# Two transformer blocks on one core: POOL's square roots moved ahead of its weight work, one operation of the rotation moved to ScalarE, the mean correction moved to VectorE, and multiplications of zeros before the first FFN

## The chip, the cores and the metric

One core of one Trainium2 chip. The metric is device time in microseconds (us); lower is better. Engines: PE is TensorE, with PEld for its weight loads, DVE is VectorE, ACT is ScalarE, POOL is GpSimd, SP is SyncE (here it issues DMAs). Each has its own instruction stream, runs it in order, and waits for the others through semaphores.

## The reference

Four sequences of 256 tokens of width 256, float32, through two blocks:

```python
xn = layernorm(x)
x = x + attn0(xn, w_norm, w_qkv, w_out, pm) + ffn0(xn, weight, bias, gamma, beta)
xn = layernorm(x)
x = x + attn1(xn, w_qkv, w_o) + ffn1(xn, w_fc, w_proj)
```

`attn0` has windows of two tokens with 16 learned keys. `ffn0` is one ternary matrix. `attn1` has 32 query heads and 4 key/value heads of 64, with rotary positions, causal:

```python
def _rope(x, pos):
    x1, x2 = jnp.split(x, 2, axis=-1)
    return jnp.concatenate([x1 * cos - x2 * sin, x2 * cos + x1 * sin], axis=-1)
```

`ffn1` is layer norm, quantized input, ternary 256 x 1024, exact GELU, layer norm again, ternary 1024 x 256.

## The kernel before

The order of every engine is written out by hand, with semaphores between the engines. To keep float32 accuracy with the fast matmul format, operands are split: ACT writes a rounded half (`hi`), and another engine subtracts it from the full value (`lo`).

**Front.** PE makes the products of block 0's attention and ffn (`g_products`, `m_products`, `ffn_0(b)`, `attention_0(b)`); DVE adds each batch to x (`add0(b)`) and takes its layer statistics (`stats1(b)`); POOL raises the variance to -1/2 (`batch_root(b)`, through `root`, L593); ACT normalises (`normal1(b)`, L473); PE transposes (`turn_tokens(b)`); ACT and DVE split the result (`tokens_hi`, `tokens_lo`). Beside this ACT turns weights ternary (`sign`, L407), sums |w_proj| (L452) and rounds the attention weights in 18 parts (`weights_hi`, L463), from which POOL makes `lo` parts (`weights_lo`, L607), in the same order.

**FFN of block 1.** Ten steps, a tile of 128 tokens in each. PE: `hidden_T(t)`, `fc(step)` (L1114), `proj(t-1)` (L1138) and a projection for the attention (`fill`, L1179). ACT: `hidden_hi`, `gelu`. DVE: `hidden_stats(t)`, `hidden_lo(t)`, `hidden_factors(t)` (L877, needs POOL's `tile_root(t)`), `ffn_add(t-1)` (L888). PE's `proj(t)` waits for `ffn_add(t-1)`.

**Attention of block 1.** 16 iterations (batch, key head) of 6 slots; 96 slots in all. In slot n PE makes scores of unit n (L1229), transposes the probabilities of unit n-2 (L992), multiplies a group of units by the values (L1266), and at some slots projects the outputs (L1286) or fills bank 6 with a new projection. ACT's slot: `probs_T(n-2)` (L528), exponents `probs(n)` (L519), group copy, `raw` copy of the fill (L494). DVE's slot: `maxima(n)` (L910), `normalise(n-1)` (L926), `probs_lo(n-2)` (L932), group `lo`.

**Rotation.** The fills are 36 blocks of queries or keys, 32 of them from slots: a q block at slots 6it and 6it+3, a k block at slots 10, 34 and 58. For block n: `raw` copy on ACT, SP moves the half heads (`turned`, four DMAs), POOL multiplies twice (`rope_products`, L648 and L650), then in `rope_sums` writes the sum rounded (`split_hi`, L658), the sum full (L659), and the difference (`split_lo`, L660); SP places both (`place_heads`, four DMAs for q, eight for k). Buffers are double: the `raw` copy of block n waits for the products of block n-2. A q block is used 9 slots after its fill. In its loop POOL takes after each of blocks 4 to 11 up to two weight parts and one `mean_part` (L671 and L674: x += wcol * factor, for the mean that the second layer norm subtracts).

Of the kernel before, what the change touches and what calls it, by code (L numbers as in the profile page):

```python
# [9 lines left out]
BF16 = mybir.dt.bfloat16  # L10
# [4 lines left out]
P = 128  # L15
# [15 lines left out]
UNITS = 6  # L31
# [34 lines left out]
def build(nc, seq, w_qkv0, w_out0, pm, w_ffn0, bias0, w_qkv1, w_o1, w_fc, w_proj, vec, const, out):  # L66
    with ExitStack() as ctx:
# [36 lines left out]
        def at(name, offset, shape, dt=F32):  # L104
# [58 lines left out]
        mcol = at("mcol", 187 * K, [P, DIM])  # L163
# [16 lines left out]
        lo0_done = sem("lo0_done")  # L180
        tern_in, nb_done, ones_done, wcol_full, wcol_done, f_mean, mean_made = (
            sem(n) for n in ("tern_in", "nb_done", "ones_done", "wcol_full", "wcol_done", "f_mean", "mean_made"))
# [12 lines left out]
        raw_done, rope_done, split_done = sem("raw_done"), sem("rope_done"), sem("split_done")  # L195
# [15 lines left out]


# [4 lines left out]
        def fills_at(it, u):  # L217
# [8 lines left out]
            if u == 4 and g == 2 and b + 1 < B:  # L226
# [4 lines left out]
        HI_IN = {0: 4, 1: 5, 2: 6, 3: 7, 4: 8, 5: 9, 6: 10, 7: 12}  # L231
# [4 lines left out]
                + [f for it in range(ITS) for u in range(UNITS) for f in fills_at(it, u)])  # L236
        PREPARED = sum(map(len, FILLS_IN.values()))
# [160 lines left out]
        def _(act):  # L398
# [25 lines left out]
            def whole_x(b):  # L424

                for k in range(KC):
# [18 lines left out]
            nc.scalar.activation(ones_r[:, :], cst[:, C_ONE:C_ONE + P], ACT.Copy).then_inc(ones_done, 1)  # L445
            act.wait_ge(p0_T, 1)
# [3 lines left out]
            sign(1, nat_fc[:, :, :], fcT[:, :, :], tern_fc)  # L450
            act.wait_ge(ld["proj"], 16)
            nc.scalar.activation(abs_out[:, :], nat_proj[:, :, :].rearrange("p c n -> p (c n)"), ACT.Abs,  # L452
                                 accum_out=wsum[:, 2:3]).then_inc(proj_sum, 1)

# [91 lines left out]
            weights_hi(0, 3)  # L546
# [32 lines left out]
        def _(pool):  # L579
# [49 lines left out]
            weights_lo(0, 2)  # L629
            batch_root(0)  # L630
            weights_lo(2, 3)
# [20 lines left out]
            def rope_sums(n):  # L652
# [13 lines left out]
            def mean_part(t):  # L666

                if t == 0:
                    pool.wait_ge(wcol_done, 1)
                pool.wait_ge(f_add, t + 1)  # L670
                pool.tensor_tensor(mcol[:, :], wcol[:, :], ffac[:, t, 4:5].to_broadcast([P, DIM]), ALU.mult).then_inc(mean_made, 1)  # L671
                pool.wait_ge(mean_made, t + 1)
                part = x[:, t // 2, t % 2, :]
                pool.tensor_tensor(part, part, mcol[:, :], ALU.add).then_inc(f_mean, 1)  # L674
                pool.wait_ge(f_mean, t + 1)

            batch_root(3)
            weights_lo(3, 4)
            tile_root(0)
            weights_lo(4, 5)  # L680
            pool.wait_ge(ld["rope"], 16)
            rope_products(0)
            tile_root(1)
            rope_sums(0)
            tile_root(2)
            rope_products(1)
            tile_root(3)
            rope_sums(1)
            tile_root(4)
            rope_products(2)  # L690
            tile_root(5)
            rope_sums(2)
            weights_lo(5, 6)
# [4 lines left out]
            weights_lo(6, 9)  # L698
# [9 lines left out]
        def _(dve):  # L708
# [27 lines left out]

            dve.memset(blk_k[:, :], 0.0).then_inc(blk_zero, 1)
# [627 lines left out]
```

## Time and profile before

| | us |
|---|---|
| median of 3 runs | 406.86 (406.72 to 406.94) |
| the profiled execution | 406.81 |
| its span | 405.0 |
| PE busy | 369.5 (91%) |
| DVE busy | 303.5 (75%) |
| POOL busy | 285.9 (71%) |
| ACT busy | 251.1 (62%) |

The chain that ended last is PE for 66% of the span, POOL for 18%, DVE for 6%. Times in rows are from the start of the span. "Idle before" and the name behind the arrow tell how long an engine waited and what ended the wait. Matmuls are pipelined, so successive starts, not the lengths of single ones, give their pace. The granted clock is a share of 2.4 GHz: 1.00 is 2.4 and 0.50 is 1.2 GHz.

### The profile page before, as it was taken

Reading aid. Unit: us, or ns where it says so; the run is one execution under the profiler, and the core shown is the slowest. Engines: PE = TensorE matmul, PEld = TensorE weight load, DVE = VectorE, ACT = ScalarE, POOL = GpSimd, SP = SyncE. Lnnn points to the kernel's source line nnn. Section 1 sums busy time; section 2 is a strip of 40 time slices with the busy share of each in tenths; the row PEclk is TensorE's granted clock in tenths of the full one; section 3 lists DMA queues with packets and bytes.
Section 4 is the critical chain, followed back from the end, with each engine's and each line's share of the span. In section 5 each row is a group of like instructions: output and inputs, shape, how many; then the busy total and the mean of one; then the engine's idle time right before and its main releaser. Section 6 shows DMA issues by size and latency. Waiting matters only on the chain.

```text
span 405.0 us, 8415 instructions
## 1 busy us (share of the span) xinstructions
PE 369.5 (91%) x2852; PEld 347.6 (86%) x2868; DVE 303.5 (75%) x675; ACT 251.1 (62%) x808; POOL 285.9 (71%) x250
## 2 busy tenths in 40 slices
PE   3994686999999979699999999999999999999995
PEld 1664574999889979699999999999999999998985
DVE  4876596786787658467977887787778778787883
ACT  1346466347598465466776757677775758677671
POOL 3445337647999999999877987677798867777000
PEclk9998699899999989879999999999999999999999
DMA  8995010522333333534434563443447344433200
GB/s 262 413 408 217 1 32 21 130 55 68 79 89 94 81 77 81 135 84 95 116 79 104 137 161 91 100 104 91 100 113 180 88 98 95 110 85 78 79 2 26
DMA packets 34219, 45.15 MB, mean 111 GB/s; under 512 B 5505, under 2 KB 25986, under 8 KB 33794
## 3 DMA queue, kind: packets, MB, share of 16 engines
q1 hardware_dynamic: 34032, 44.62, 41.2%
q8 instruction: 23, 0.38, 0.4%
q14 instruction: 18, 0.15, 0.1%
q10 hardware_dynamic: 146, 0.00, 0.0%
HBM read 13.14 MB, written 1.05 MB: 35 GB/s over the span
## 4 chain that ended last, share of the span: by engine, by line
PE 66%; POOL 18%; DVE 6%; ACT 3%; issue 3%; DMA 3%; SPq 1%; POOLq 0%
PE bank L1266 14%; PE bank L1229 11%; PE bank L992 10%; PE bank L1286 10%; PE bank L1179 9%; PE bank L1138 3%; POOL woT_lo L607 2%; PE bank L1114 2%; POOL split_lo L660 2%; POOL split_hi L658 2%; POOL rope_b L650 2%; POOL rope_a L659 2%; POOL qkvT_lo L607 2%; PE bank L1232 2%; POOL rope_a L648 2%
## 5 line engine op out<-in xcount | busy, mean ns | idle before, releaser
L519 ACT ACTIVATE bank<-bank,neg_max 128x256 f32<-128x256 f32 (+1 forms) x256 | 101.3, 397 | 6.0 <-DVE neg_max L910 5.8
L528 ACT ACTIVATE probT_hi<-bank 128x512 fp32r<-128x512 f32 x96 | 57.6, 600 | 74.2 <-PE bank L992 74.1
L910 DVE TENSOR_REDUCE neg_max<-bank 128x2 f32<-128x512 f32 (+1 forms) x96 | 66.0, 688 | 38.2 <-PE bank L1232 26.7
L1266 PE MATMUL bank<-probT_hi,v 128*128 128x256 f32 x384 | 76.7, 296 | 3.1 <-DVE probT_lo L932 2.4
L1229 PE MATMUL bank<-kT,qT 128*128 128x256 f32 (+1 forms) x512 | 75.1, 280 | 3.2 <-DMA qT<-split_lo 3.2
L650 POOL TENSOR_TENSOR rope_b<-turned,cst 128x512 f32<-128x512 f32 x36 | 46.4, 1290 | 36.2 <-DMA turned<-raw 36.1
L1229 PEld LDWEIGHTS bank<-kT,qT 128*128 128x128 f32 x512 | 68.3, 196 | 3.4 <-DMA qT<-split_lo 3.4
L932 DVE TENSOR_TENSOR probT_lo<-bank,probT_hi 128x512 fp32r<-128x512 f32 x96 | 65.4, 681 | 5.3 <-ACT probT_hi L528 5.2
L926 DVE TENSOR_TENSOR prob<-bank,rsum 128x512 f32<-128x512 f32 x96 | 66.4, 691 | 3.3
L1266 PEld LDWEIGHTS bank<-probT_hi,v 128*128 128x128 f32 x384 | 58.8, 190 | 6.2 <-DVE probT_lo L932 3.8
L992 PE MATMUL bank<-cst,prob 128*128 128x128 f32 x384 | 58.6, 276 | 3.1 <-DVE prob L926 2.1
L1266 PE MATMUL bank<-probT_lo,v 128*128 128x256 f32 x192 | 54.2, 283 | 0.0
L519 ACT ACTIVATION_READ_ACCUMULATOR bank<-bank,neg_max 128x1 f32 x256 | 53.8, 210 | 0.0
L992 PEld LDWEIGHTS bank<-cst,prob 128*128 128x128 f32 x384 | 46.6, 143 | 5.1 <-DVE prob L926 2.6
L660 POOL TENSOR_TENSOR split_lo<-rope_a,split_hi 128x512 fp32r<-128x512 f32 x36 | 46.2, 1283 | 2.8
L658 POOL TENSOR_TENSOR split_hi<-rope_a,rope_b 128x512 fp32r<-128x512 f32 x36 | 46.2, 1284 | 2.5
L648 POOL TENSOR_TENSOR rope_a<-raw,cst 128x512 f32<-128x512 f32 x36 | 46.4, 1289 | 0.6
L659 POOL TENSOR_TENSOR rope_a<-rope_a,rope_b 128x512 f32<-128x512 f32 x36 | 46.4, 1289 | 0.0
L938 DVE TENSOR_TENSOR oT_lo<-bank,oT_hi 128x256 fp32r<-128x256 f32 x64 | 27.2, 425 | 18.4 <-ACT oT_hi L533 18.3
L494 ACT ACTIVATE raw<-bank 128x512 f32<-128x512 f32 x36 | 21.8, 606 | 28.5 <-PE bank L1179 20.0
L1266 PEld LDWEIGHTS bank<-probT_lo,v 128*128 128x128 f32 x192 | 36.4, 190 | 0.0
L1179 PE MATMUL bank<-xT_hi,qkvT_hi 128*128 128x256 f32 x144 | 30.7, 295 | 2.9 <-DVE x L822 2.9
(155 smaller groups left out, 746.5 us busy)
## 6 DMA issues: line engine op xcount, KB each, us to landing
turned<-raw SPq DMA_DIRECT2D x144, 64.0 KB, 2.0
qT<-split_hi SPq DMA_DIRECT2D x64, 128.0 KB, 2.4
qT<-split_lo SPq DMA_DIRECT2D x64, 128.0 KB, 2.4
wq0T<-in_L_attn_w_qkv_dram SPq DMA_DIRECT2D x4, 512.0 KB, 8.2
wout<-in_L_attn_w_out_dram SPq DMA_DIRECT2D x4, 512.0 KB, 12.7
nat_qkv<-in_L_attn_w_qkv_dram SPq DMA_DIRECT2D x2, 1024.0 KB, 20.9
nat_o<-in_L_attn_w_o_dram SPq DMA_DIRECT2D x1, 2048.0 KB, 21.6
kT<-split_hi SPq DMA_DIRECT2D x16, 128.0 KB, 2.4
```

The lines of the kernel that those rows point to most:

```text
L519: ins = nc.scalar.activation(own, own, ACT.Exp, bias=neg_max[it % 2][:, first + j:first + j + 1], accum_out=sums[it % 2][:, first + j:firs ...
L528: nc.scalar.activation(probT[0][:, n % 4, :], bank[2 + n % 2][:, :], ACT.Copy).then_inc(t_hi, 1)
L648: pool.tensor_tensor(a, whole, cos, ALU.mult)
L650: own_done(pool.tensor_tensor(z, half, sin, ALU.mult))
L659: own_done(pool.tensor_tensor(a, a, z, ALU.add))
L910: dve.tensor_reduce(neg_max[n // UNITS % 2][:, unit_columns(n % UNITS)], score_bank(n)[:, :].rearrange("p (h k) -> p h k", h=heads), AX.X, ...
L926: dve.tensor_tensor(a, e, share, ALU.mult).then_inc(s_norm, 1)
L932: dve.tensor_tensor(lo, bank[2 + n % 2][:, :], hi.bitcast(F32), ALU.subtract).then_inc(t_lo, 1)
L992: ins = pe.transpose(ps[:, P * j:P * j + P], a, ident)
L1179: ins = pe.matmul(bank[place][:, SEQ * j:SEQ * j + SEQ], qkvT[w][:, k, at:at + P], xT[s][:, k, SEQ * b:SEQ * b + SEQ], start=i == 0, stop= ...
L1229: pe.matmul(ps[:, keys * j:keys * j + keys], qT[it % 2][:, h + j, P * c:P * c + P], kT[b % 2][:, g, s, 0:keys], start=j == 0 and s == 0, s ...
L1266: ins = pe.matmul(group_bank(), v[b % 2][:, DH * z:DH * z + P], p, start=m == 0, stop=m == last)
```

## The change

1. POOL takes `weights_lo` in other portions: one part before the root of batch 0, two before that of batch 1, and later parts between roots. The root of batch 3 comes behind parts 3 and 4.
2. ACT takes one weight part before `sign(1)` and the absolute sum, two after; the load of the GELU table comes before `probT0`.
3. DVE adds batches 2 and 3 to x before `hidden_scale(0)` and `tokens_lo(0)`. `hidden_factors` stands one step later, right before `ffn_add`.
4. From block 4 on ACT, not POOL, writes `split_hi`, as a copy of POOL's full sum, in the slot four after the block's fill, between `probs_T` and `probs`. POOL waits for it before `split_lo`. Blocks 0 to 3 stay as they were.
5. `mean_part` becomes one DVE operation at the head of slots 6 to 13.
6. PE multiplies a zeroed tile of 512 columns (bfloat16) into unused banks: 14 times at the start, 6 times before and 5 times after the transposes of batch 0, which now stand behind `ffn_0(3)` and `attention_0(3)`.

```diff
@@ ScalarE
+            nc.scalar.activation(table_use[:, 0:1], table_use[:, 1:2], ACT.Gelu)
             act.wait_ge(p0_T, 1)
...
+            def high_rotated(n):
+                act.wait_ge(rope_done, summed(n))
+                if n >= 2:
+                    has_landed(act, n - 2)
+                nc.scalar.activation(split[0][:, n % 2, :, :], rope_a[:, n % 2, :].rearrange("p (j t) -> p j t", j=2),
+                                     ACT.Copy).then_inc(split_hi, 1)
             def slot(n):
                 if 2 <= n < N_UNITS + 2:
                     probs_T(n - 2)
+                for f in BLOCKS[OWN_HIGH:]:
+                    if FILL_SLOT[f] + 4 == n:
+                        high_rotated(BLOCK[f])
...
-            nc.scalar.activation(table_use[:, 0:1], table_use[:, 1:2], ACT.Gelu)
-            weights_hi(0, 3)
+            weights_hi(0, 1)
+            sign(1, nat_fc[:, :, :], fcT[:, :, :], tern_fc)
+            act.wait_ge(ld["proj"], 16)
+            nc.scalar.activation(abs_out[:, :], nat_proj[:, :, :].rearrange("p c n -> p (c n)"), ACT.Abs,
+                                 accum_out=wsum[:, 2:3]).then_inc(proj_sum, 1)
+            weights_hi(1, 3)
@@ GpSimd
-            weights_lo(0, 2)
+            weights_lo(0, 1)
             batch_root(0)
-            weights_lo(2, 3)
+            weights_lo(1, 3)
...
-                pool.tensor_tensor(hi, a, z, ALU.add)
+                if n < OWN_HIGH:
+                    pool.tensor_tensor(hi, a, z, ALU.add)
                 own_done(pool.tensor_tensor(a, a, z, ALU.add))
+                if n >= OWN_HIGH:
+                    pool.wait_ge(split_hi, n - OWN_HIGH + 1)
                 pool.tensor_tensor(lo, a, hi.bitcast(F32), ALU.subtract).then_inc(split_done, 1)
...
-                weights_lo(2 * n + 1, min(2 * n + 3, len(W_UNITS)))
-                if n - 4 < TILES:
-                    mean_part(n - 4)
+                weights_lo(2 * n + 2, min(2 * n + 4, len(W_UNITS)))
@@ VectorE
+            dve.memset(idle_in[:, :], 0.0).then_inc(idle_ready, 1)
...
             stats1(1)
+            add0(2)
+            add0(3)
             hidden_scale(0)
...
+                dve.scalar_tensor_tensor(part, wcol[:, :], ffac[:, t, 4:5], part, ALU.mult, ALU.add).then_inc(f_mean, 1)
             def slot(n):
+                if 6 <= n < 6 + TILES:
+                    mean_part(n - 6)
...
-                    hidden_factors(t)
+                if t >= 1:
+                    hidden_factors(t - 1)
+                    ffn_add(t - 1)
@@ TensorE
+            def keep_busy(b, count):
+                for _ in range(count):
+                    pe.matmul(bank[b][:, :], idle_in[:, 0:P], idle_in[:, :], start=True, stop=True)
+            pe.wait_ge(idle_ready, 1)
+            keep_busy(5, 14)
...
-            turn_tokens(0)
             ffn_0(3)
             attention_0(3)
+            keep_busy(4, 6)
+            turn_tokens(0)
+            keep_busy(2, 5)
```

## Rows read from the trace of the kernel before

**Rows 1.** Stages: stretch, length, busy us (instructions) of PE, PEld, DVE, ACT, POOL; clock; DMA

```profile
34.00:42.00 8.00, 1.36 (x7) 0.82 (x6) 5.50 (x19) 5.13 (x9) 4.81 (x5) 0.67 0.17 72
...
52.00:67.50 15.50, 14.89 (x96) 12.75 (x96) 11.55 (x39) 12.81 (x24) 8.92 (x9) 1.00 0.14 35
67.50:71.20 3.70, 0.01 (x1) 0.05 (x1) 3.63 (x7) 1.26 (x2) 3.05 (x3) 0.95 0.00 0
...
76.10:106.00 29.90, 29.90 (x225) 28.42 (x222) 21.59 (x58) 17.74 (x34) 21.21 (x20) 1.00 0.27 62
...
176.50:405.00 228.50, 222.21 (x1852) 215.98 (x1862) 178.99 (x360) 152.75 (x544) 159.34 (x127) 1.00 0.41 97
```

**Rows 2.** The chain that ended last, front: start us, length us, engine, tile, line

```profile
39.59 0.98 POOL tok L593
...
46.54 2.10 PE bank L1114 x8
...
71.19 3.49 PE bank L1138 x16
...
76.12 0.87 PE bank L992 x8
...
78.85 1.90 PE bank L1138 x16
```

**Rows 3.** Timeline, 25 to 40 us: start us, length us, engine, line, operation

```profile
27.49 0.59 ACT L447 ACTIVATE probT<-bank 64x512 f32<-64x512 f32 x1 [1.39 <-PE bank L1082]
...
31.10 2.00 ACT L407 ACTIVATE fcT<-nat_fc,neg_magic 128x2048 fp32r<-128x2048 f32 x1 [1.36 <-DVE nat_fc L773]
...
34.80 0.16 DVE L719 TENSOR_SCALAR tok<-tok 128x2 f32<-128x2 f32 x1
...
35.02 1.28 ACT L545 ACT_TABLE_LOAD   x1
...
36.42 1.65 ACT L463 ACTIVATE qkvT_hi<-nat_qkv 128x512 fp32r<-128x512 f32 x3
```

**Rows 4.** Timeline of POOL and of DVE, the same moment

```profile
40.79 1.26 POOL L607 TENSOR_TENSOR qkvT_lo<-nat_qkv,qkvT_hi 128x512 fp32r<-128x512 f32 x1
...
40.79 1.28 DVE L841 TENSOR_TENSOR tok<-tok 128x2 f32<-128x2 f32 x1
```

**Rows 5.** Groups by line: busy us, mean ns of one, idle before and its releaser

```profile
L650 POOL TENSOR_TENSOR rope_b<-turned,cst 128x512 f32<-128x512 f32 x36 | 46.4, 1290 | 36.2 <-DMA turned<-raw 36.1
...
L494 ACT ACTIVATE raw<-bank 128x512 f32<-128x512 f32 x36 | 21.8, 606 | 28.5 <-PE bank L1179 20.0 <-POOL rope_b L650 8.5
...
L607 POOL TENSOR_TENSOR woT_lo<-nat_o,woT_hi 128x512 fp32r<-128x512 f32 x8 | 10.2, 1283 | 0.0
...
L674 POOL TENSOR_TENSOR x<-x,mcol 128x256 f32<-128x256 f32 x8 | 5.9, 735 | 0.6
...
L671 POOL TENSOR_TENSOR mcol<-wcol,ffac 128x256 f32<-128x256 f32 x8 | 4.9, 613 | 0.0
...
L888 DVE SCALAR_TENSOR_TENSOR x<-bank,ffac,x 128x256 f32<-128x256 f32 x8 | 3.8, 481 | 5.2 <-PE bank L1138 5.2
```

**Rows 6.** Timeline of PE in the attention: slots 13, 14, a wait, slot 15, slot 21

```profile
138.23 0.64 PE L1229 MATMUL bank<-kT,qT 128*128 128x256 f32 x4
...
140.71 1.01 PE L1229 MATMUL bank<-kT,qT 128*128 128x128 f32 x8
...
144.80 0.50 PE L1266 MATMUL bank<-probT_hi,v 128*128 128x256 f32 x2 [2.41 <-DVE probT_lo L932]
...
146.65 1.80 PE L1229 MATMUL bank<-kT,qT 128*128 128x128 f32 x8
...
170.93 1.97 PE L1229 MATMUL bank<-kT,qT 128*128 128x128 f32 x8 [3.21 <-DMA qT<-split_lo]
```

**Rows 7.** Timeline of ACT, a `raw` copy in the attention

```profile
142.94 0.60 ACT L494 ACTIVATE raw<-bank 128x512 f32<-128x512 f32 x1 [4.87 <-POOL rope_b L650]
```

**Rows 8.** Timeline of POOL, before its loop over the later blocks

```profile
105.21 2.51 POOL L607 TENSOR_TENSOR qkvT_lo<-nat_qkv,qkvT_hi 128x512 fp32r<-128x512 f32 x2
```

More of the change, by code:

```diff
@@ L162, in build @@
         wcol = at("wcol", 186 * K, [P, DIM])
-        mcol = at("mcol", 187 * K, [P, DIM])
+        idle_in = at("idle_in", 187 * K, [P, 512], BF16)
         abs_out = at("abs_out", 164 * K, [P, FF // P * DIM])
@@ L194, in build @@
         v_zero = sem("v_zero")
-        raw_done, rope_done, split_done = sem("raw_done"), sem("rope_done"), sem("split_done")
+        raw_done, rope_done, split_done, split_hi = sem("raw_done"), sem("rope_done"), sem("split_done"), sem("split_hi")
         turn_landed = [sem(f"turn_landed{i}") for i in range(2)]
@@ L209, in build, with summed @@
         STEPS = TILES + 2
+        def summed(n):
+            return 2 * n + 2
         def of_batch(it):
@@ L236, in build @@
                 + [f for it in range(ITS) for u in range(UNITS) for f in fills_at(it, u)])
+        OWN_HIGH = sum(f[0] != "v" for fs in FILLS_IN.values() for f in fs)
+        FILL_SLOT = {f: UNITS * it + u for it in range(ITS) for u in range(UNITS) for f in fills_at(it, u)}
         PREPARED = sum(map(len, FILLS_IN.values()))
@@ L664, in tile_root @@
                 root(ffac[:, t:t + 1, 1:2], t + B + 3)
[L666 to L675, printed above, removed]
+            weights_lo(3, 5)
             batch_root(3)
-            weights_lo(3, 4)
-            tile_root(0)
-            weights_lo(4, 5)
             pool.wait_ge(ld["rope"], 16)
             rope_products(0)
+            tile_root(0)
+            rope_sums(0)
             tile_root(1)
-            rope_sums(0)
+            weights_lo(5, 6)
+            rope_products(1)
             tile_root(2)
-            rope_products(1)
+            rope_sums(1)
             tile_root(3)
-            rope_sums(1)
+            weights_lo(6, 7)
+            rope_products(2)
             tile_root(4)
-            rope_products(2)
+            rope_sums(2)
             tile_root(5)
-            rope_sums(2)
-            weights_lo(5, 6)
+            weights_lo(7, 9)
             tile_root(6)
@@ L697, in _ @@
             rope_sums(3)
-            weights_lo(6, 9)
+            weights_lo(9, 10)
             for n in range(4, len(BLOCKS)):
@@ L945, in add_out, with mean_part @@
                 dve.tensor_tensor(dst, dst, bank[BANK_OUT][:, :].rearrange("p (e n) -> p e n", e=2), ALU.add).then_inc(out_added, 1)
+            def mean_part(t):
+                if t == 0:
+                    dve.wait_ge(wcol_done, 1)
+                dve.wait_ge(f_add, t + 1)
+                part = x[:, t // 2, t % 2, :]
+                dve.scalar_tensor_tensor(part, wcol[:, :], ffac[:, t, 4:5], part, ALU.mult, ALU.add).then_inc(f_mean, 1)
             def slot(n):
+                if 6 <= n < 6 + TILES:
+                    mean_part(n - 6)
                 if n % (HKV * UNITS) == UNITS and n > HKV * UNITS:
@@ L959, in slot @@
                     empty(fills_at(n // UNITS, n % UNITS))
-            add0(2)
             stats1(2)
             tokens_lo(1)
-            add0(3)
             stats1(3)
@@ L977, in _ @@
                     hidden_scale(step + 1)
-                if t >= 1:
-                    ffn_add(t - 1)
                 empty(FILLS_IN.get(step, ()))
```

12 lines of the change are left out of this document (4 added, 8 removed).

## The prediction

> **What bounds the kernel now.** I read the stages first, then the chain, then the single waits. The stage table [rows 1] shows a kernel that TensorE (PE) bounds in two long stretches, 76.1 to 106 us (busy 29.90 of 29.90) and 176.5 to the end (222.21 of 228.50, the rest mostly at its tail). Only what stands before 76.1 us and between 138 and 176 us can be shortened by reordering.
>
> In front, PE is busy 1.36 us of 34 to 42 and 0.01 us of 67.5 to 71.2 [rows 1]. The chain [rows 2] says why. The root of batch 0 starts at 39.59, while VectorE (DVE) had its argument at 34.80 + 0.16 = 34.96 [rows 3]: GpSimd (POOL) takes `weights_lo(0, 2)` first, and these wait for ScalarE (ACT), which is behind `sign(1)`, the absolute sum and a table load of 1.28 us. The first `fc` then starts at 46.54. The second hole is circular: DVE stands at `hidden_factors(1)` until POOL has taken `tile_root(1)`, which is queued behind weights and rotation; PE waits for the `ffn_add` behind it. The projection that follows takes 3.49 us for 16 matmuls where a later one takes 1.90 [rows 2]: its clock fell to 1.2 GHz after the hole.
>
> In the attention POOL is the late one. A block with two weight parts and a mean part costs it 5 x 1.29 + 2 x 1.28 + 0.61 + 0.74 = 10.4 us [rows 5], while PE asks for one about each 8.7 us (two per iteration; an iteration is 17.4 us when nothing waits). PE meets that as 2.41 us at 144.80 and 3.21 us at 170.93 [rows 6], the first through ACT, whose `raw` copy waited 4.87 us for a rotation [rows 7].
>
> **Roots first and the heating matmuls: -10.4 us.** Three steps.
>
> (a) ACT keeps only one weight copy ahead of `sign(1)`. It falls into the 1.36 us that ACT waits there anyway [rows 3]; the table load goes into the 1.39 us before `probT0` and overshoots by about 0.1, which nobody waits for. Both are costed at nothing; without their covers they would be 0.5 and 1.3 us. ACT then ends sum and two copies at 36.1. POOL has no weights pending, roots at 35.0, and `normal1(0)` starts at 36.3 (before: 39.59 + 1.3). That is 4.5 us.
>
> (b) `y1` is written at 37.4. PE is then in `ffn_0(3)`, `attention_0(3)` and `keep_busy(4, 6)`. A 512-column matmul is 2.10/8 = 0.26 us [rows 2], so six are up to 1.6 and end near 38.5; the transposes wait about a microsecond for them. That is what the heating costs, and it brings a warm clock: the eight products of `ffn_0(3)` and the four transposes ran cold before. ACT copies, and DVE reaches `tokens_lo(0)` at 41.0, because `add0(2)`, `add0(3)` and `hidden_scale(0)` are now queued ahead of it. First `fc` at 41.7: 4.8 us earlier.
>
> (c) Up to the transposes of tile 3 (76.12 before [rows 2]) PE and POOL no longer hold anybody: the roots have a whole step, as `hidden_factors` stands one step later, and `ffn_add(0)` needs no late root. What is late next is DVE. From 52 to 67.5 it is busy 11.55 of 15.5 us [rows 1], and from `tokens_lo(0)` to `hidden_lo(2)` it has about 20 us of work, 1 us of waiting for others, and some three port waits of about 1 us. So 41.7 + 24 = 65.7, and 76.1 - 65.7 = 10.4 us. Bounds: 12 with no port wait, 8.5 with five.
>
> DVE and POOL hinder one another: a two-column product took 1.28 us while POOL ran a subtraction of 1.26 us from the same instant [rows 4].
>
> The 14 matmuls at the start cost nothing on the path: 14 x 0.26 x 2 = 7.3 us at the lower clock at most, and the first `g_products`, 3.6 us even then, end before or at 10.7 us or so, when the next weights have landed; bound 0 to 1. The zeroing of `idle_in` runs in DVE's wait for `pm`. From 76.1 to 106 PE is the bound in both kernels: no change.
>
> **The attention: -4.1 us, then +2.6.** POOL loses the sum it wrote as `split_hi` (1.29) and the mean parts (0.61 + 0.74), and starts the loop with one weight part where three stood (-2.5 us of the three that run from 105.21 on [rows 8]; the other two are taken earlier, in POOL's waits). A block costs it 4 x 1.29 + 2 x 1.28 = 7.7 us, later 5.2, below PE's 8.7.
>
> But the copy now sits in ACT's queue at the slot four after the fill, between `probs_T` and `probs`. It waits for POOL's sum, and everything ACT does waits with it; in turn POOL's `split_lo` waits for ACT's slot. Fills come three slots apart except the k blocks, which come one slot after a q block. Slot 13 to 14 is 140.71 - 138.23 = 2.48 us [rows 6]. Between the two copies POOL must do `split_lo`, two weights, two products and a sum: 1.28 + 2.56 + 2.58 + 1.29 + about 0.3 = 8.0 us. On the clock of the kernel before: copy of block 7 at 139.9, sum of block 8 at 148.0, ACT at that copy from 142.9, so it stands 5.2 us. PE needs the result two slots on, at 140.71 + 2 x 2.95 + 0.6 = 147.2; it gets it after the copy (0.5), four exponents (1.4) and DVE's reciprocal and product (0.95), at 150.9: idle 3.75 us, and a cold stretch behind it. After 2.41 us of idling eight score matmuls took 1.80 us for 1.01 [rows 6]; after the two longer waits the loss was 1.6 (3.49 - 1.90) to 2.7 us. I take 2. The first k block costs 5.8 us.
>
> The mean parts add 8 x 0.48 us to DVE in slots 6 to 13 (by the `ffn_add` form [rows 5]), and both its inputs lie in SBUF, so each can wait for POOL as in [rows 4]: 0 to 1.28 us. With half of that, 8 x 1.1 = 9 us goes into some 5 us of idle time and 2 us of pipeline; I add 1.2 us (0 to 4). The SBUF — State Buffer page of the Trainium skill (Who interferes with whom) says the second of two such operations blocks fully until the first ends; the rows agree, and with every mean part meeting a whole POOL operation its rule would put the DVE term near 4 us, 2.8 above mine.
>
> In the kernel before, slots 14 to 20 would last 21.8 us at the lengths that the same slots have one iteration later, so slot 21 would start at 162.5 and not at 170.93 [rows 6], and it took 2.7 us longer than 2.95 itself: 11.1 us lost. 11.1 - 7.0 = 4.1 us are won.
>
> The later k blocks (slots 34 and 58) have no weights between: 5.4 us of POOL work from one copy to the next sum, against 2.5 us plus ACT's place in its slot. ACT stands 2.7 us, of which some 1.4 is slack: 1.3 us of PE each, 2.6 in all, where the kernel before had none. Bounds: 0, and 4 each if the clock falls too. The 32 copies themselves (0.6 us as the `raw` copy [rows 5], 0.5 in spacing) lie in ACT's waits for PE: at nothing; on the path they would be 16 us.
>
> **Sum.** Profiled execution 406.81 (span 405.0 and 1.8 around it; the median, 406.86, is the same): 406.8 - 10.4 - 4.1 + 2.6 = 394.9. The k blocks' DMAs (eight in SP's queue, ahead of the next `turned`) can hold the next block by about 1 us more; I say 395.5.
>
> **Rivals.**
> *A, POOL and ACT never hold PE.* The copies find their sums ready, k blocks included: 406.8 - 10.4 - 11.1 = 385.3, to 389 with small waits. For it: POOL's load falls below PE's pace. Against: the 8.0 us in a 2.5 us gap. 14%.
> *B, the new wait is a second POOL bound.* Each k block cools PE and delays the next two blocks through SP: 8, 4 and 4 us, front gain at 8.5: 406.8 - 8.5 - 3.1 + 8 = 403.2. For it: the 3.2 us wait was enough for the lower clock. Against: later k blocks carry no weights. 18%.
> *C, slower: the copy lands on the path in every block.* ACT does the copy between two steps of the loop scores, exponent, share, transposes; if the loop has less than 0.5 us slack, 28 to 32 copies cost 14 to 16 us: 395.5 + 14 = 409.5. It decides at about 0.4 us per copy. Against: PE is nearly gapless from 176.5 on [rows 1] with ACT busy 152.75 of 228.5. 5%.
> *D, the front wins nothing net:* the roots come early but the clock stays low and DVE stays the bound: 406.8 - 3 - 4.1 + 2.6 = 402 to 406.5. 4%.
>
> **How the numbers follow.** The forecast (389 to 401) has 59%. The range to hold 8 in 10 reaches into A and B: 388.5 to 401.5. The measurement can tell about 0.2% (0.8 us) from no change. Faster by more: 0.92; within: 0.02; slower: 0.06.
>
> **What would show it.** The root of batch 0 at 35 us and `normal1(0)` near 36.3; the first `fc` near 41.7; no PE wait over 2 us from 42 to 66, and the 16 projections of tile 1 at 1.9 us; the transposes of tile 3 near 65.7. In the attention `raw` waits for no rotation; instead ACT's copy into `split_hi` waits for POOL's sum, longest (about 5 us) at the first k block, near 132 us on the new clock, and 2 to 3 us at the two others. Wrong would be: PE holes spread over all blocks (C), or none (A).

## The result, and the profile after

The change made the kernel slightly slower, by 0.6%: 409.6 us median (408.28 to 411.75) against 407.02 (406.34 to 409.5) for the kernel before beside it, a ratio of 1.0056, 95% interval [1.0032, 1.008]. The forecast was 395.5 with a range of 388.5 to 401.5. The profiled execution took 410.91 us, its span is 409.1 (before: 406.81 and 405.0), so it lies 1.3 us above its median, and the one before 0.2 below.

The first and the last scores of the attention split the span into three parts. From the timeline of PE, the kernel before and then the kernel after (start us, length us, engine, line, operation; slots 0 and 95):

```profile
101.18 0.52 PE L1229 MATMUL bank<-kT,qT 128*128 128x256 f32 x3
...
390.92 0.64 PE L1229 MATMUL bank<-kT,qT 128*128 128x256 f32 x4
```

```profile
94.20 0.52 PE L1256 MATMUL bank<-kT,qT 128*128 128x256 f32 x3
...
395.05 0.52 PE L1256 MATMUL bank<-kT,qT 128*128 128x256 f32 x3
```

The attention begins 7.0 us earlier and takes 300.85 us instead of 289.74, 11.1 more; 11.1 - 7.0 = 4.1 us, which is all of the difference between the two profiled executions. So the front won two thirds of what was forecast, and the attention, which should have won 1.5 us, lost 11.1.

The stages in front and the tail of the attention, the first two the same stretches as in [rows 1], the last from slot 23 to the end (in the kernel before slot 23 starts at 179.06, and from 176.50 to there PE has no gap):

```profile
34.00:42.00 8.00, 7.70 (x45) 5.44 (x43) 7.55 (x24) 5.38 (x9) 5.87 (x7) 1.00 0.15 63
52.00:67.50 15.50, 12.10 (x78) 11.11 (x77) 14.91 (x37) 10.74 (x19) 13.13 (x12) 0.89 0.36 83
...
170.10:409.10 239.00, 224.47 (x1843) 216.63 (x1841) 176.82 (x357) 164.71 (x566) 122.94 (x97) 0.99 0.38 91
```

PE now works through 34 to 42 us, 2.7 us of it on the eleven zero multiplications. From 52 to 67.5 DVE is the one nearly without a gap (14.91 of 15.50). And the stretch that PE had bounded (222.21 of 228.50) now has 14.5 us in which PE stands, 6.3 before.

Who waited for whom, in total us, times, longest (waits of the kernel after):

```profile
POOL split_lo L679 <- ACT split_hi L541: 94.4, 32, 4.9
...
DVE oT_lo L948 <- ACT oT_hi L534: 39.4, 47, 6.8
...
PE bank L1010 <- DVE prob L936: 13.6, 7, 5.4
...
ACT split_hi L541 <- POOL rope_a L676: 11.2, 3, 5.5
...
ACT raw L495 <- PE bank L1206: 9.8, 16, 2.1
...
PE bank L1293 <- DVE oT_lo L948: 4.9, 11, 0.7
...
PE bank L1010 <- DVE hT_lo L892: 3.4, 1, 3.4
```

`raw` waits for no rotation any more (8.5 us of such waits in [rows 5]). But ACT waits three times for POOL's sum, 11.2 us in all, and PE behind it through DVE's `prob`; and PE has eleven short waits for `oT_lo`, 4.9 us in all, where the kernel before had two, 0.6 us. POOL's own 94.4 us cost nothing by themselves: they only say that it stands in 32 meetings instead of being free.

**The three long holes.** A hole is a stretch in which PE stands. The first is in slot 16. Timeline of POOL, ACT, DVE and PE, 137 to 149 us:

```profile
137.47 2.54 POOL L623 TENSOR_TENSOR woT_lo<-nat_o,woT_hi 128x512 fp32r<-128x512 f32 x2
...
142.58 1.26 POOL L676 TENSOR_TENSOR rope_a<-rope_a,rope_b 128x512 f32<-128x512 f32 x1
143.87 0.63 ACT L541 ACTIVATE split_hi<-rope_a 128x512 fp32r<-128x512 f32 x1 [5.51 <-POOL rope_a L676]
144.41 0.32 ACT L520 ACTIVATE bank<-bank,neg_max 128x128 f32<-128x128 f32 x1
...
145.78 0.39 ACT L534 ACTIVATE oT_hi<-bank 128x256 fp32r<-128x256 f32 x1
...
146.20 0.42 DVE L948 TENSOR_TENSOR oT_lo<-bank,oT_hi 128x256 fp32r<-128x256 f32 x1 [6.78 <-ACT oT_hi L534]
146.54 0.68 DVE L920 TENSOR_REDUCE neg_max<-bank 128x4 f32<-128x512 f32 x1
...
147.34 0.69 DVE L936 TENSOR_TENSOR prob<-bank,rsum 128x512 f32<-128x512 f32 x1
...
148.09 1.12 PE L1010 MATMUL bank<-cst,prob 128*128 128x128 f32 x4 [5.36 <-DVE prob L936]
```

Read it downwards, each line lets go of the next. POOL is late with the sum because the k block follows one slot behind a q block, and here two weight parts lie between them. Behind the copy stand, in ACT's order, four exponents and the group copy `oT_hi`; DVE, also in order, stands at `oT_lo` for that copy, and has `neg_max` of the next unit queued ahead of `prob`. From the end of the sum to the end of `prob` it is 148.03 - 143.84 = 4.2 us. The four transposes on PE then take 1.12 us, where at the full clock they take 0.60. Slot 16 lasts 10.87 us, and 3.91 without a hole. The same at the second k block (slot 40), where no weights lie between:

```profile
221.39 0.63 ACT L541 ACTIVATE split_hi<-rope_a 128x512 fp32r<-128x512 f32 x1 [2.86 <-POOL rope_a L676]
...
225.61 0.66 PE L1010 MATMUL bank<-cst,prob 128*128 128x128 f32 x4 [2.75 <-DVE prob L936]
...
226.21 0.78 PE L1293 MATMUL bank<-probT_hi,v 128*128 128x256 f32 x2
```

ACT stands 2.86 us and PE 2.75, so the slack between them is 0.1 us; the matmuls behind run at the lower clock (0.78 us where 0.48 and 0.40 are usual). Slot 40 lasts 8.59 us, slot 64 8.57, for 3.91.

**The single copies.** Slot 23, an ordinary one, timeline of PE:

```profile
171.78 0.48 PE L1293 MATMUL bank<-probT_hi,v 128*128 128x256 f32 x2 [0.48 <-DVE oT_lo L948]
```

The slot takes 3.91 us (170.10 to 174.01) where it took 3.41 before (179.06 to 182.47). Nine of the sixteen last slots of an iteration are longer like this, 4.3 us in all.

### The profile page after: what moved, and what is told of

Its sections match the earlier page's. It is cut to its first block, busy times and chain, and to the rows that moved or that the text cites. A ratio compares the mean times of both kernels' runs of the same rounds, so it can differ in the third digit from the quotient of the medians.

```text
span 409.1 us, 8530 instructions
## 1 busy us (share of the span) xinstructions
PE 376.0 (92%) x2893; PEld 348.9 (85%) x2893; DVE 311.6 (76%) x684; ACT 269.2 (66%) x840; POOL 235.3 (58%) x202
## 4 chain that ended last, share of the span: by engine, by line
PE 54%; ACT 15%; DVE 12%; POOL 11%; issue 6%; DMA 2%; SPq 0%; POOLq 0%; ACTq 0%; DVEq 0%
PE bank L1293 10%; PE bank L1010 8%; ACT bank L520 8%; PE bank L1313 7%; PE bank L1206 7%; PE bank L1256 6%; PE bank L1165 4%; PE bank L1141 3%; POOL rope_b L666 3%; POOL rope_a L676 3%; ACT split_hi L541 3%; POOL rope_a L664 2%; POOL split_lo L679 2%; DMA wq0T<-in_L_attn_w_qkv_dram 2%; DVE neg_max L920 2%
## 5 line engine op out<-in xcount | busy, mean ns | idle before, releaser
L679 POOL TENSOR_TENSOR split_lo<-rope_a,split_hi 128x512 fp32r<-128x512 f32 x36 | 46.1, 1280 | 94.7 <-ACT split_hi L541 94.4
L1293 PE MATMUL bank<-probT_hi,v 128*128 128x256 f32 x384 | 79.1, 302 | 4.9 <-DVE oT_lo L948 4.9
L1256 PE MATMUL bank<-kT,qT 128*128 128x256 f32 (+1 forms) x512 | 73.3, 276 | 0.0
L1293 PEld LDWEIGHTS bank<-probT_hi,v 128*128 128x128 f32 x384 | 60.8, 196 | 8.5 <-issue 6.8
L1256 PEld LDWEIGHTS bank<-kT,qT 128*128 128x128 f32 x512 | 66.6, 191 | 0.0
L1293 PE MATMUL bank<-probT_lo,v 128*128 128x256 f32 x192 | 55.3, 288 | 0.0
L1293 PEld LDWEIGHTS bank<-probT_lo,v 128*128 128x128 f32 x192 | 37.6, 196 | 0.0
L1259 PE MATMUL bank<-mask_b,ident_b 128*128 128x256 bf16 (+1 forms) x96 | 30.6, 319 | 0.0
L1206 PE MATMUL bank<-xT_hi,qkvT_lo 128*128 128x256 f32 x144 | 29.0, 283 | 0.0
```

The lines of the kernel that those rows point to most:

```text
L1206: ins = pe.matmul(bank[place][:, SEQ * j:SEQ * j + SEQ], qkvT[w][:, k, at:at + P], xT[s][:, k, SEQ * b:SEQ * b + SEQ], start=i == 0, stop= ...
L1256: pe.matmul(ps[:, keys * j:keys * j + keys], qT[it % 2][:, h + j, P * c:P * c + P], kT[b % 2][:, g, s, 0:keys], start=j == 0 and s == 0, s ...
L1293: ins = pe.matmul(group_bank(), v[b % 2][:, DH * z:DH * z + P], p, start=m == 0, stop=m == last)
```

## The experiments

"The base" is from here on the kernel after with every rounded half left on POOL (the first experiment). The times of the kernel before are those beside each run.

| kernel | us | ratio to before, 95% | slot 0 | slots 0 to 95 |
|---|---|---|---|---|
| before | 407.02 | | 101.18 | 289.74 |
| after | 409.6 | 1.0056 [1.0032, 1.008] | 94.20 | 300.85 |
| halves on POOL (base) | 392.7 | 0.9658 [0.964, 0.9676] | 95.47 | 281.13 |
| base, second | 390.95 | 0.959 [0.9547, 0.9632] | 92.59 | 281.10 |
| base, third | 390.1 | 0.9568 [0.954, 0.9596] | 92.61 | 281.54 |
| base, mean parts on POOL too | 396.61 | 0.9705 [0.9655, 0.9755] | 93.65 | 285.64 |
| k halves alone on POOL | 410.99 | 1.0048 [1.0023, 1.0074] | 93.75 | 301.62 |
| copy at the end of its slot | 397.77 | 0.973 [0.9687, 0.9773] | 92.28 | 288.23 |
| copies spaced | 401.31 | 0.9828 [0.9775, 0.9881] | 92.64 | 291.49 |
| both, no 14 zeros | 395.65 | 0.972 [0.9693, 0.9747] | 93.44 | 286.68 |
| five slots behind the fill | 407.33 | 0.9985 [0.9959, 1.0012] | 95.36 | 297.67 |
| every copy twice | 421.48 | 1.0335 [1.0293, 1.0376] | 94.28 | 311.02 |
| base, mean parts spread | 391.55 | 0.9591 [0.9556, 0.9626] | 94.46 | 281.88 |
| mean parts on POOL too, no zeros | 401.14 | 0.9861 [0.9846, 0.9875] | 97.98 | 287.14 |
| mean parts on POOL too, no 14 zeros | 397.2 | 0.9757 [0.9708, 0.9806] | 95.83 | 288.93 |
| base with 20 first zeros | 389.99 | 0.9552 [0.9527, 0.9578] | 92.77 | 281.03 |
| base with no first zeros | 393.55 | 0.9618 [0.958, 0.9656] | 92.64 | 281.21 |

The last two columns are starts of the scores of slot 0 and the length from there to slot 95, each from the profiled execution. The kernel before had medians of 406.88 to 408.8 beside these runs, so kernels are best compared by their ratios. The median 397.2 leaves out one run of 400.66 us, more than 1.5% above the fastest of its kernel, and that run is the profiled one.

### Take the copy back, alone

The base: the loop of copies goes, and POOL writes `split_hi` again for all blocks; the mean parts stay on DVE.

```diff
-                for f in BLOCKS[OWN_HIGH:]:
-                    if FILL_SLOT[f] + 4 == n:
-                        high_rotated(BLOCK[f])
-                if n < OWN_HIGH:
+                if True:
                     pool.tensor_tensor(hi, a, z, ALU.add)
-                if n >= OWN_HIGH:
-                    pool.wait_ge(split_hi, n - OWN_HIGH + 1)
```

> The changed kernel with every split_hi written by POOL, as before, but the mean parts still on DVE. Against x3_front_only (span 393.4), where the mean parts are on POOL too, it prices the mean parts' move alone. Theory 7 (both its inputs lie in SBUF, so it waits for POOL's operations, 0.5 to 1.5 us each in the profile, in a stretch where DVE has little idle time): slots 5 to 13 get 1.4 to 1.8 us longer; but POOL saves 1.35 us in each of the blocks in which it bounds slots 13 to 21, which gives back up to what x3_front_only loses there (7.3 us over ideal slots). Span 388 to 392 if POOL's saving counts. Rival (DVE's loss is the larger): 394 to 396.

The attention falls from 300.85 to 281.13 us: the moved copy costs 19.7 us of it. Slot by slot that is 7.0 + 4.7 + 4.7 for the three holes, 4.3 for the nine single copies, 0.5 in slots 12 and 13, and 1.4 given back at slot 20, where PE now waits for a placed block. All that POOL's fuller load costs PE is that one wait. Waits of the base (third run), PE's longest:

```profile
PE bank L1005 <- DVE hT_lo L887: 3.4, 1, 3.4
PE bank L1005 <- DVE prob L931: 2.7, 4, 0.9
PE bank L1014 <- DMA wq0T<-in_L_attn_w_qkv_dram: 1.9, 1, 1.9
PE bank L1251 <- DMA qT<-split_lo: 1.6, 1, 1.6
```

and POOL's largest group still stands 42.5 us for DMAs:

```profile
L663 POOL TENSOR_TENSOR rope_b<-turned,cst 128x512 f32<-128x512 f32 x36 | 47.1, 1308 | 42.5 <-DMA turned<-raw 42.5
```

Then also the mean parts go back to POOL, two operations each:

```diff
-                if 6 <= n < 6 + TILES:
-                    mean_part(n - 6)
+                if n - 4 < TILES:
+                    mean_part(n - 4)
```

> The front of the changed kernel (roots first, order of ACT and DVE, zeros on PE) with the attention of the kernel before: POOL writes every split_hi and makes the mean parts. Slot 1 starts 7 us earlier than before in either case. Theory 1 (the whole loss lies in what was moved to ACT and DVE): the span is 405.0 - 7.1 = 398 or less; less if POOL, which enters its loop with fewer weights pending, holds PE for less than the 2.4 and 3.2 us of before: down to 393. Rival 4 (the front's gain is given back anyway, since POOL bounds slots 12 to 21 and sets the pace from there): 402 to 405.

285.64 us: the mean parts on POOL cost 4.5 (slots 14 and 16 at 4.77 and 7.37 us, for 2.94 and 3.91). What is left between this and the kernel before, 4.1 us, is the other portioning of the weights and the earlier start. In these profiled executions 289.74 - 4.1 - 4.5 (mean parts) + 19.7 (copy) = 300.85.

The 19.7 and the 8.6 that the weights and the mean parts make together are measured against a base that repeats: its attention took 281.10 to 281.54 us in three executions. How the 8.6 splits is less certain. The attention's code is the same in the two kernels without zeros below, and there it took 287.14 and 288.93 us, with all of the difference in slots 0 and 16 to 21. Timeline of PE, slot 21, with all the zeros and then without the 14:

```profile
161.91 1.11 PE L1263 MATMUL bank<-kT,qT 128*128 128x128 f32 x8 [1.30 <-DMA qT<-split_lo]
```

```profile
164.72 1.97 PE L1262 MATMUL bank<-kT,qT 128*128 128x128 f32 x8 [3.14 <-DMA qT<-split_lo]
```

The second is like slot 21 of the kernel before [rows 6]. By these executions the mean parts on POOL cost 4.5 to 7.8 us and the portions are worth 0.8 to 4.1.

### Where the copy stands

First only the k blocks, whose wait made the holes, back to POOL:

```diff
-                    if FILL_SLOT[f] + 4 == n:
+                    if f[0] == "q" and FILL_SLOT[f] + 4 == n:
```

> The changed kernel, but for the three later k blocks POOL writes split_hi itself again; the 29 q blocks stay on ACT. Theory 1 (ACT stands at the copy of a k block for POOL's sum, and nothing behind it has slack): the three holes of PE (5.36, 2.75 and about 2.8 us) and the slow clock behind each go, 4.7 us each at the second and third, 5 to 7 at the first: span 409.1 - 9.3 - 6 = about 394. Rival 2 (POOL is late at these blocks whoever rounds, and PE would be held by the raw copy or by the placing instead, as before): it gains half at most, span 401 to 404. Rival 3 (the copies themselves are what costs, in every block): only 3 of 32 copies go, span 408 to 409.

A miss: 410.99 us. The holes moved one slot on, to 17, 41 and 65 (10.61, 7.77 and 7.27 us for 3.18), to the copy of the q block behind the k block. Timeline of PE in this kernel:

```profile
152.30 0.77 PE L1294 MATMUL bank<-probT_hi,v 128*128 128x256 f32 x2 [5.64 <-DVE oT_lo L949]
```

Its sum is now behind the k block's five operations. My first theory, that the k block's own copy is the trouble, fell: whichever copy comes next waits for all that POOL still owes.

Then the same copies, moved within ACT's order: to the end of their slot (behind `probs` and the group copy), to slots that leave more room around the k blocks (five slots behind the fill for each k block and for the q block behind it), and both.

```diff
                 if n < N_UNITS:   # end of the slot
+                for f in BLOCKS[OWN_HIGH:]:
+                    if FILL_SLOT[f] + 4 == n:
+                        high_rotated(BLOCK[f])
                     empty(fills_at(n // UNITS, n % UNITS))
```

> The changed kernel with ACT's copy at the end of the same slot, behind the exponents and the group copy. Theory 1: the exponents no longer wait for it. The 0.5 us that each iteration loses (about 3.7 in all) goes, the holes at the second and third k block go (2.9 us of standing, now in front of nothing urgent: -9), the first shrinks from 5.4 to about 2.5 us: span 393 to 397. Rival 2 (it is POOL's lateness, wherever the copy stands): holes stay, span 405 to 409.

```diff
+        HIGH_SLOT = {f: s + (5 if f[0] == "k" or s % 24 == 12 and s < 72 else 4) for f, s in FILL_SLOT.items()}
-                    if FILL_SLOT[f] + 4 == n:
+                    if HIGH_SLOT[f] == n:
```

> The changed kernel with the copy of a k block one slot later (five after its fill) and that of the q block behind it also five after its fill, so that the copies around a k block stand two slots apart instead of one, then three; the place inside the slot is unchanged. Theory 1: POOL needs 5.4 us from copy to next sum, two slots are 5 to 6 us: the second and third hole go (-9.3), the first shrinks by one slot of 2.9 us (8 us of work, weights included) and leaves 2 to 3 us of it: span 395 to 398. Rival 2: the later placing makes the score matmuls wait for qT or kT instead: 400 to 409.

> The changed kernel without the first 14 zeros, with both mends: the copy at the end of its slot, and the copies around a k block spaced out (k five slots after its fill, the next q block five too). Theory 1, with what x1_keys_on_pool added (the copy must stand where POOL's sum is ready, for every block near a k block, and must not stand ahead of the exponents): no hole over 1 us at slots 40 and 64, the one at slot 16 under 3 us, no loss of 0.5 us per iteration: span 387 to 391. Rival (placing too late, score matmuls wait for qT): holes at slots 21, 45 and 69, 392 to 397.

At the end of its slot a copy holds nobody: of the nine long slots seven are as in the kernel before, the other two at 3.53, and the holes shrink to 4.9, 1.2 and 1.2 us, because the exponents go out first. Spaced, the two later holes vanish (slots 40 and 64 at 3.90 and 3.91) and the first is 2.1, but the single copies stay (3.90 to 4.06), and slots 22, 45, 46, 69 and 70 are 0.5 to 1.0 us longer than in the base, 4.0 us together. With both (and without the 14 zeros at the start, which lie ahead of the attention) it is 286.68 us. That was a miss too: the span is 394.2 us, not 387 to 391, because slots 22, 44, 46 and 70 lose 0.7 to 1.3 us each, 4.0 together. At 22, 46 and 70 PE waits for DVE's `prob` in both kernels; what holds that was not followed further. So a better place in the order was worth 12 to 14 of the 19.7 us, and still the best placed copy is 5.5 us behind no copy.

Last, every copy one slot later, the distances between them unchanged:

```diff
-                    if FILL_SLOT[f] + 4 == n:
+                    if FILL_SLOT[f] + 5 == n:
```

> The changed kernel with every moved copy five slots after its block's fill instead of four; the distances between successive copies stay one and three slots. Theory 1 (the gap between two successive copies decides, because POOL may start the remaining work of the k block only after the copy of the q block before it): the holes stay and move one slot on, to slots 17, 41 and 65, of about 5.0, 2.4 and 2.4 us (a slot of 2.9 instead of 2.5 us now lies between the two copies), and the time stays at 407 to 411. Rival 2 (a copy stands too near to its own fill, so it asks for the sum before POOL can have it): each of the three waits shrinks by a whole slot, 2.5 to 2.9 us, ACT's longest wait for POOL's sum falls from 5.5 to 2.6 us, the later two vanish with their cold stretches, and the time falls by 9 to 12 us to 398 to 401.

ACT's longest wait is 5.08 us where it was 5.51, not 2.6: POOL may begin the k block's remainder only after the copy of the q block ahead, so a later copy finds POOL equally late. That is theory 1. Its place was half a miss: PE's hole stayed in slot 16, now in front of a projection, which wants the bank that ACT's `raw` empties:

```profile
148.27 0.63 ACT L541 ACTIVATE split_hi<-rope_a 128x512 fp32r<-128x512 f32 x1 [5.08 <-POOL rope_a L676]
...
150.83 0.80 PE L1222 MATMUL bank<-qkvT_hi,xT_hi 128*128 128x256 f32 x2 [4.39 <-ACT raw L495]
```

The attention is 3.2 us shorter than with four slots, since this wait has 0.7 us of slack (5.08 against 4.39), and a single copy costs 0.2 and 0.1 us in two slots instead of 0.5 in one; slots 8, 14 and 41 give 0.9 to 1.5 us each back.

### The price of the copy itself

```diff
+                nc.scalar.activation(spare[:, :, :], rope_a[:, n % 2, :].rearrange("p (j t) -> p j t", j=2), ACT.Copy)
                 nc.scalar.activation(split[0][:, n % 2, :, :], rope_a[:, n % 2, :].rearrange("p (j t) -> p j t", j=2),
```

> The changed kernel with each of the 32 moved copies done twice on ACT, first into a spare tile and then as before. Theory 1 (in the slot that each iteration gives to the first q block's copy nothing is slack, in the slot of the other q block something is): about 14 copies and the 3 of the k blocks put their full 0.5 us on the path, 8.5 us in all, 418 us, with the slots 5, 11, 17 ... at 4.4 us where they are 3.90 now; if the other 15 have no slack either, 16 us, 425. Rival 2 (the copy itself hides, only the wait for POOL's sum costs): within 2 us of the changed kernel, 411, and those slots stay at 3.90.

The attention grows by 10.2 us. The nine long slots grow by another 0.5 each (slot 23: 173.30 to 177.71, 4.41), 4.6 us together, and the holes by 1.5, 2.0 and 0.9. In a slot of ACT's order that has no slack a copy costs its spacing in full, and so does a second one; the other slots showed nothing but 1.1 us in slots 9 to 12. I had expected 8.5: fourteen single copies on the path (there are nine) and one copy in each hole (they deepened by two to four).

### The mean parts

```diff
-                if 6 <= n < 6 + TILES:
-                    mean_part(n - 6)
+                if n % UNITS == 5 and 3 <= n // UNITS < 3 + TILES:
+                    mean_part(n // UNITS - 3)
```

> The changed kernel with every rounded half left on POOL, and the eight mean parts of DVE no longer at the head of slots 6 to 13 but one in each of iterations 3 to 10, at their last slot. In the kernel with the mean parts at 6 to 13 slot 10 took 5.17 us for 3.9 and the port waits fell into slots where DVE is late. Theory 1 (DVE's mean parts cost because they follow one another): slot 10 falls by 1.0 to 1.3 us, the later slots 5, 11, 17 ... pay 0 to 0.2 each, and the time is 391.0 to 392.0 against 392.7. Rival 2 (each costs the same wherever it stands, about 0.3 us): 392.7 again, or up to 394 where DVE is late at the end of an iteration.

> The changed kernel with every rounded half left on POOL, as run before, beside the kernel with the spread mean parts on the same chip: 392.7 us, 0.4 either way. It is the base for a difference of less than one per cent.

Slot 10 fell from 5.17 to 3.90 us as expected, but slots 24, 42 and 66, each right behind a mean part, grew by 0.6 to 0.9 us. The ratios are equal, 0.9591 and 0.959, so spreading gives nothing, as rival 2 had it. The base itself came out 1.8 us lower than expected; in the profiled executions its front is the reason (slot 0 at 92.59 for 95.47, the attention the same), which the next part takes up.

### The zeros in front

With the mean parts and the halves on POOL, first all zeros out, then only the 14 at the start:

```diff
-            keep_busy(5, 14)
-            keep_busy(4, 6)
-            keep_busy(2, 5)
```

> x3_front_only without any multiplication of zeros (its span was 393.4). Theory 5 (the zeros hold the clock up before the first fc, and are worth something there): the 6 and 5 zeros cost PE about 1.3 us before the transposes of batch 0 but keep them and the first fc at 2.4 GHz; without them PE is idle from about 38.4 on, waits of 1 to 3 us stand instead, and the span is 0 to 2 us longer. Rival 5 (the edit's front gain is all order, since DVE is what is late there): no more than 0.5 us difference either way, 393 to 394.

> x3_front_only without the 14 zeros at the start alone. In the profiled execution of the changed kernel PE had a 2.77 us hole behind them, and the 24 products of the attention weights then took 7.08 us against 5.39 in the kernel before; in four other executions with the 14 zeros the hole was 1.5 to 2.4 us and the products took 5.39. Theory 6 (the zeros finish the first products too early and so open a hole that now and then costs the clock): the median falls by 0 to 1 us and the spread is smaller. Rival 6 (they do nothing on average): same within 0.5 us.

Without any, slot 0 starts at 97.98 and the time is 401.14 us (0.9861); without the 14, 95.83 and 397.2 (0.9757); with all 25, 93.65 and 396.61 (0.9705). Both expectations missed: the span without any is 5.8 us longer where 0 to 2 was expected, and leaving out the 14 did not lower the median. The 6 and 5 around the first transposes are worth some 2 us at slot 0 (95.83 to 97.98), and 4 by the medians: without them the first `fc` waits 3.42 us instead of 1.4 and runs at the lower clock (0.77 us for 0.48).

What the 14 bring is a matter of chance. Timeline of PE at the start, kernel after and then the base (third):

```profile
1.19 4.76 PE L1042 MATMUL bank<-idle_in 128*128 128x512 bf16 x14 [1.19 <-DVE idle_in L744]
...
10.59 7.08 PE L1019 MATMUL bank<-wq0T,blk_k 128*64 128x256 f32 x24 [2.77 <-DMA wq0T<-in_L_attn_w_qkv_dram]
```

```profile
1.19 5.68 PE L1037 MATMUL bank<-idle_in 128*128 128x512 bf16 x14 [1.19 <-DVE idle_in L739]
...
10.69 5.39 PE L1014 MATMUL bank<-wq0T,blk_k 128*64 128x256 f32 x24 [1.95 <-DMA wq0T<-in_L_attn_w_qkv_dram]
```

The same 14 took 4.49 to 5.97 us; the eight products behind them then end sooner or later, and the next 24, which wait for weights, meet a long or a short hole. In the profiled kernels with 14 zeros a hole of 2.66 to 3.12 us went with 7.08 us for the 24, one of 1.5 to 2.44 with 5.39. So the next kernels have six more zeros, and none:

```diff
-            keep_busy(5, 14)
+            keep_busy(5, 20)
```

> The kernel with every rounded half on POOL, with 20 zero multiplications at the start instead of 14. In the runs so far the 14 took 4.49 to 5.97 us; where 1.5 to 2.4 us of nothing stood between the eight products after them and the next 24, these took 5.39 us, where it was 2.66 to 3.12 they took 7.08. Theory 1 (the hole before the 24 products makes the lower clock): six more of 0.26 us close the hole to 0.8 to 1.5 us, the 24 products take 5.39 us, and the scores of slot 0 start at 92.6 as in the faster of the two profiled runs of the base (95.5 in the other); the time is 1 to 1.5 us below the base run beside it. Rival 2 (what differs between those runs is not the hole): the 24 products take 7.08 again in this run or its base alike, and the times are equal within 0.5 us; or the longer zeros delay the first products, which adds 0 to 1 us.

> The kernel with every rounded half on POOL, without the 14 zero multiplications at the start (the 6 and 5 around the first transposes stay). Theory 1 (the first products run at the lower clock without them, 3.65 us for eight, and the next 24 as the clock then stands, 5.39 or 8.3 us as seen): with 5.39 the front is as early as with the zeros, with 8.3 it is 2.9 us later; 391 to 394 us, so the 14 zeros are worth 0 to 3 us. Rival 2 (they bring nothing on the path): equal to the base within 0.5 us.

> The kernel with every rounded half on POOL once more, as the base on the same chip for the two with 20 and with none of the zeros: 391 to 393 us; its 24 products take 5.39 or 7.08 us, by the hole before them (under or over 2.5 us).

With 20 the hole was 1.48 us, the 24 took 5.39, and the times lie within 389.69 to 390.04. With 14 beside it they lie within 389.52 to 391.67, with none within 389.75 to 394.16, at 389.75 and 390.64 or from 393.12 up. The median with 20 is that of the 14, and theory 1's gain of 1 to 1.5 us in the median did not come. A narrower spread with 20 is suggested and not shown: there are four runs of it, and with 14 four of six lie at 390.18 or below. The version with 20, 389.99 us, is 4.5% below the kernel before, [0.9527, 0.9578], and no run sets it apart from the base beside it.

The hole alone does not decide. Timeline of PE without the 14, in two kernels whose fronts are the same:

```profile
10.83 8.35 PE L1026 MATMUL bank<-wq0T,blk_k 128*64 128x256 f32 x24 [1.77 <-DMA wq0T<-in_L_attn_w_qkv_dram]
```

```profile
10.49 5.39 PE L1014 MATMUL bank<-wq0T,blk_k 128*64 128x256 f32 x24 [1.76 <-DMA wq0T<-in_L_attn_w_qkv_dram]
```

The hole is the same to 0.01 us, and the 24 products take 8.35 or 5.39 us. In five executions without the 14, the kernel before among them, the holes were 1.48 to 1.91 us, and the products took 5.39 three times and 8.29 and 8.35 once each. So that a long hole makes the lower clock is only a fit to the kernels with zeros; what decides stays open.

## Why the prediction was wrong

**The front, -10.4 said, -7.0 measured: right mechanism, too large.** The order of events came as described. Timeline of the kernel after: POOL's root and ACT's normalise; PE's first `fc`; three DVE operations that POOL delays; PE at the hole and at tile 3:

```profile
36.63 1.01 POOL L609 TENSOR_TENSOR tok<-tok,neg_half 128x4 f32<-128x4 f32 x1 [1.60 <-DVE tok L726]
...
37.95 1.09 ACT L474 ACTIVATE y<-x,tok 128x256 f32<-128x256 f32 x2 [0.32 <-POOL tok L633]
```

```profile
43.17 0.48 PE L1141 MATMUL bank<-fcT,xT_hi 128*128 128x512 f32 x1 [1.40 <-DVE xT_lo L858]
```

```profile
50.67 2.32 DVE L781 TENSOR_SCALAR nat_proj<-nat_proj,winv 128x2048 f32<-128x2048 f32 x1
...
57.49 0.98 DVE L849 TENSOR_TENSOR tok<-tok 128x2 f32<-128x2 f32 x1
58.51 1.21 DVE L850 SCALAR_TENSOR_TENSOR ffac<-tok,wscale 128x2 f32<-128x2 f32 x1
```

```profile
56.27 1.94 PE L1010 MATMUL bank<-cst,ffn_h 128*128 128x128 f32 x8 [3.40 <-DVE hT_lo L892]
...
68.77 1.23 PE L1010 MATMUL bank<-cst,ffn_h 128*128 128x128 f32 x8
```

The root came at 36.63 (said 35), the first `fc` at 43.17 (said 41.7), tile 3's transposes at 68.77 (said 65.7). The step that failed first is "the 14 matmuls at the start cost nothing on the path; bound 0 to 1": the 24 products behind them ran partly at the lower clock and took 7.08 us for 5.39, 1.7 us. In the second run of the base, where they took 5.39, the first `fc` starts at 41.61, as said, and slot 0 is 8.6 us earlier than before. Since the products can take 8.3 us without the 14 too, the term left out is the clock at these products, and not the zeros for certain. The second is "from `tokens_lo(0)` to `hidden_lo(2)`", with "some three port waits" (DVE standing for an operation of POOL): the profile shows at least four (2.32 us for a scaling that took 1.73 earlier in the same kernel, 0.98 for 0.16, 1.21 for 0.22, and 1.17 for 0.17 at 49.51), PE stands 3.40 us at the transposes of tile 1, and these take 1.94 us for 1.06. I had said that no PE wait would be over 2 us there. That hole of 3.4 us is in every kernel with this front; that DVE's order, not POOL, makes it was read, not tried.

**The attention's relief, -11.1 + 1.2 = -9.9 said, -8.6 measured: near.** POOL no longer holds PE in the stretch where it did, but for 1.4 us at slot 20 of the base. The part that failed is what it was put down to: removing `split_hi` from POOL was not needed for it. The base keeps it, and its attention takes 281.1 us. The weights' portions and the mean parts, 8.6 us together, were enough.

**The mean parts on DVE, +1.2 said, 1.3 measured** (slot 10, 5.17 for 3.91). The size came out right in part by luck: it was said of eight slots, and one slot paid it all. The group of the kernel after:

```profile
L963 DVE SCALAR_TENSOR_TENSOR x<-wcol,ffac,x 128x256 f32<-128x256 f32 x8 | 8.4, 1045 | 0.0
```

8.4 us for eight that take 0.48 each undisturbed, so 4.6 us of waiting for POOL's operations, of which about 1.3 reached PE. The rule of the Trainium skill that I had weighed (SBUF — State Buffer, Who interferes with whom) is that the second of two such operations stands until the first ends. The trace agrees: the eight took 0.47 to 1.62 us, so none waited longer than the 1.28 us of one POOL operation. By the prediction's estimate the path would have paid near 4 us if each had met a whole operation; they met half of one on average, and DVE had room for most of it.

**The k blocks, 5.8 + 1.3 + 1.3 said, 7.0 + 4.7 + 4.7 measured: the step that failed.** ACT's waits were right, 5.51 us for 5.2 and 2.86 for 2.7. Wrong was what I made of them. Of the wait of 2.7 us, "some 1.4 is slack"; by the rows it is 0.1. And the path behind the copy was "the copy, four exponents, DVE's reciprocal and product", 2.85 us; the rows show 4.2, with the group copy on ACT, `oT_lo` and the next unit's maxima in DVE's order between. At the later two I also left out the lower clock behind the hole, which I had charged at the first; it is some 2 of the 4.7. This is nearly rival B's price (8, 4 and 4), which had 18%, but not its path: B let the delay go through SP to the next two blocks, and slots 17 to 22 are as short here as in the base or shorter.

**The 32 copies, 0 said, 4.8 measured.** "They lie in ACT's waits for PE" holds for those in slots with slack. In nine slots of the kind of slot 23 each costs its 0.5 us of spacing. That is rival C's mechanism in under a third of the blocks. I had let it count only for all blocks or for none, and only instead of B. Both happened together: 406.8 - 7.0 - 8.6 + 16.3 + 4.8 - 1.4 = 410.9, the profiled execution (16.3 are the holes, 1.4 what slot 20 gave back). The busy share that spoke against C (152.75 of 228.5 us) says how much ACT works, not whether it works in the moment at which PE's data pass through it.

## What to carry to other kernels

An operation that is moved to an engine in the middle of a loop brings a meeting with it: ask what stands behind it in both in-order queues, down to the engine that bounds, and count each of those operations, before calling a wait slack. The wait at a meeting is set by what the other engine owes since the last meeting, so look for the two that follow closest, and expect the wait to go to the next one if only that one is removed. Relieve an engine first of work that nobody waits for (here the weights' portions and the mean parts, 8.6 us); see whether it is still late before paying for more.

## What the runs showed of the hardware that I had not expected

The clock's rise and fall is not the same from run to run. 14 equal multiplications took 4.49 to 5.97 us, and the 24 products behind them 5.39 or 7.08. In two executions of the base slot 0 started at 95.47 and at 92.59. Of these 2.9 us the products made 1.6 (first `fc` at 43.17 and 41.61). The other 1.3 came behind the same hole of 3.40 us: in the one, `fc` multiplications went on at 0.63 us each, where in the other they took 0.39; the kernel after, with its first `fc` at 43.17 too, had slot 0 at 94.20. A hole of 2.41 us before [rows 6] and the ones of 5.36 and 2.75 after each left PE at the lower clock, and slots 16 and 40 lost another 1.6 and 1.9 us by it (6.96 - 5.36 and 4.69 - 2.75). And a DVE operation of two columns, 0.16 us alone, took 0.98 beside a POOL operation of 1.27: six times its length, where the long scaling of 1.73 us became 2.32.
